# Moving the output's wait behind a branch, marking the branch on every engine, and new order tables in a graph-network kernel

## The chip, the cores and the metric

One core of a Trainium2 chip runs the kernel. The metric is the device time of one execution in microseconds, of which the median of three runs is taken. The engines are PE (matmul; its weight loads are PEld), DVE (vector), ACT (scalar), POOL (GpSimd) and SP (Sync), which issues all DMAs here.

## What is computed

128 graphs of 128 nodes with 64 features go through two layers, each followed by x + layer(x) and a layer norm.

```python
# layer 0
mask = (adj > 0.0)
h = relu((x @ W1a)[:, :, None, :] + (x[:, :, None, :] - x[:, None, :, :]) @ W1b + b1)   # H = 192
hm = einsum('bjkh,bjk->bjh', h, mask)
x = layernorm(x + hm @ W2 + deg[..., None] * b2)
# layer 1
m = relu(relu(x @ W1 + b1) @ W2 + b2)
msg = relu(einsum('bij,bjh->bih', adj, m))
gi, gh = msg @ W_ih.T + b_ih, x @ W_hh.T + b_hh          # GRU gates r, z, n
x = layernorm(x + (1 - z) * n + z * x)
```

## The kernel before

Layer 0 is done in 32 quads of four graphs (NQ = 32). For each quad q, prep builds selection words (rank_n, off, ov, rank_t, rank_ov, words), turned inputs (x_split, x_turn) and the products V (v, v_low), which Sync stores and loads again as VA and VB. A quad then goes through nine a rounds and nine b rounds. In a round PE multiplies VA or VB by a selection matrix DM (fp8, L886 and L894) into PSUM, and DVE takes the maximum with zero and adds it to AC (round_a L1184, round_b L1205; the first a round's part is on ACT). DM comes from dgen on DVE (L1163), four per step. s_ov, out0_a, out0_b and out0_c (the "tail", L959 to L988) turn AC into layer 0's output XR. Layer 1 (layer1_steps) works on units of eight graphs, the last one in two halves: squares and POOL's power for the norm, transposes (xg), m1, m2 (L702), msg (L715), gates, tanh, h, yt, the second norm and the store (L1900).

All five engines run one program each, and main_order writes down the order of the calls once for all of them; an engine takes from it those stages that it has. Step t runs round_b of quad t-1 and round_a of quad t, in turn, with 19 slots between them. What stands in a slot is written as letters in tables: p is the next piece of prep of quad t+1, r of the ranks of a group of eight graphs, t of the tail, b of POOL's add_u and scale_u, n, d and e of layer 1 units (youngest to oldest), s seeds, 0 to 3 dgen, l load, c clear, f the checks, h a conversion of biases. HEAD orders the start: there L is the first loads, X the load of XQ, W the load of bs and wa, E of w2, K of constants, G of wg, S POOL's setup, A POOL's parts of the bias, w DVE's wide_w. FIRST is step 0, ORDER the even and odd steps 1 to 30, LAST the last two, END what is left after the rounds. An engine works strictly in order, so a letter's place decides what waits behind it.

The checks (flag) count inputs for which this path doesn't hold. Their sum is cast to fi (L1317). When the five programs are through, the block ends in a barrier (L1923); each engine loads fi (L1930), and a branch runs a dense fallback over 16 groups if fi is over 0. For this input it is 0. In the profile the branch is the COMPARE_BRANCH of bacc.py:44.

```python
            sy.wait_ge(s["out"], 16 * (NG + 1))
            sy.wait_ge(s["flag"], 3)
    ...
        over = nc.values_load(fi[:], min_val=0, max_val=768)
        with nc.If(over > 0):
            with nc.Fori(0, NG) as gv:
```

Of the kernel before, what the change touches and what calls it, by code (L numbers as in the profile page):

```python
# [23 lines left out]
NG = NB // GB  # L24
# [29 lines left out]


ORDER = (
    ("se", "2pp3", "rb", "bp", "ep", "pt", "p", "bter", "p", "td", "tp", "eeeer", "d", "p", "", "ebp", "de", "c", "0r1"),
    ("slp", "2p3", "bdbbe", "", "tdb", "tp", "", "tt", "p", "ddp", "cp", "enpdr", "npd", "ddn", "p", "d", "pd", "0r1", "dp"),
)

FIRST = ("2hsp", "b3", "", "bp", "p", "", "r", "hpb", "p", "prrr", "", "bcp", "", "r", "0", "pp", "hpp", "", "1r")

LAST = (
    ("bs2bt", "", "etttn", "b3d", "", "nd", "dn", "dbd", "nd", "d", "dd", "dnde", "", "", "d", "dn", "", "n01", ""),
    ("bbetdff", "ftte2d3", "ndtnendeeeddddd", "", "df", "edbd", "nnbe", "", "d", "", "n", "en", "", "d", "", "dfen", "", "", ""),
)

HEAD = ("LSW", "Xrc", "ArE", "rKAGp", "trrrww", "pMrrt", "pppt", "p", "tfp01pp", "p", "pA")

END = ("td", "dt", "dl", "dtdtltnnn", "dllnn", "dl", "lnl", "n", "nln", "l", "l", "nnl", "ndn", "l", "n", "n", "l", "n", "nl", "n", "ll", "ntll")  # L70

MAIN = (
# [119 lines left out]
def build(nc, adj, adjt, xt, xn, xq, w1, w2, rows, wg, cst, out):  # L192
    ctx = ExitStack()
    with ctx:
# [232 lines left out]
        def finish(steps):  # L427
            for n, _ in enumerate(steps):
                assert n < 99, "waits for a bank that nothing gives back"

        def main_order(do):
# [131 lines left out]
            for t in range(NQ + 1):  # L563
                link["t"] = tail(t - 2) if t > 1 else iter(())
                link["b"] = parts_of_u(t)
                if t % 2 == 0:
                    link["e"], link["d"] = link["d"], link["n"]
                elif t > 2:
                    link["n"] = layer1_steps(do, bank, t // 2 - 1)
                if t + 1 < NQ:  # L570
                    link["p"] = prep(t + 1)
                if t % 2 and t // 2 + 2 < NG:
                    link["r"] = ranks(t // 2 + 2)
                if t == NQ:
                    link["n"] = layer1_steps(do, bank, NG - 1)
                    link["f"] = checks()
                order = FIRST if t == 0 else ORDER[t % 2] if t < NQ - 1 else LAST[t - NQ + 1]

                def between(codes):
                    for c in codes:  # L580
                        if c in "01":
                            do("dgen", t + 1, int(c))
                        elif c in "23":
                            do("dgen", t, int(c))
                        elif c == "s":
                            do("seeds", t)
                        elif c == "c":
                            do("clear", t + 1)
                        elif c == "l":
                            if t // 2 + 2 < NG:  # L590
                                do("load", t // 2 + 2)
                        else:
                            next(link[c], 0)

                between(order[0])
                for n in range(1, 10):
                    if t:
                        do("round_b", t - 1, n)
                    between(order[2 * n - 1])
                    if t < NQ:  # L600
                        do("round_a", t, n)
                    between(order[2 * n])
                finish(link["h"])
                finish(link["p"])
                finish(link["b"])
                finish(link["f"])
                finish(link["t"])
            for k in range(2):
                do("add_u", NQ - 1, k)
            link = {"t": tail(NQ - 1), "n": link["n"], "d": link["d"]}  # L610
# [152 lines left out]
        def tensor_main(e):  # L763
# [228 lines left out]
            def fsum(b, gates):  # L992
# [8 lines left out]
            follow(main_order, {"rank_n": rank_n, "off": off, "ov": ov, "rank_t": rank_t, "rank_ov": rank_ov, "x_turn": x_turn,  # L1001
                                "v": v, "v_low": v_low, "surplus": surplus, "seeds": seeds, "round_a": round_a, "round_b": round_b,
                                "s_ov": s_ov, "out0_a": out0_a, "out0_b": out0_b, "out0_c": out0_c, "fsum": fsum,
                                **tensor_layer1(e, pe, s)})
# [118 lines left out]
        def vector_main(e):  # L1123
# [195 lines left out]
            follow(main_order, {"mask": mask, "count": count, "off": off, "words": words,  # L1319
                                "dgen": dgen, "round_a": round_a, "round_b": round_b,  # L1320
                                "wide_w": wide_w, "fold": fold, "s_ov": s_ov, "add_u": add_u, "bias": bias, "flag": flag, "fsum": fsum,
                                **vector_layer1(e, ve, s)})
# [153 lines left out]
        def scalar_main(e):  # L1476
# [149 lines left out]
            follow(main_order, {"rank_n": rank_n, "split_x": split_x, "off": off, "ov": ov, "rank_t": rank_t, "rank_ov": rank_ov,  # L1626
                                "x_split": x_split, "x_turn": x_turn, "v": v, "v_low": v_low, "surplus": surplus, "seeds": seeds, "round_a": round_a, "s_ov": s_ov, "out0_c": out0_c,
                                "fold": fold, "split_x1": split_x1, "split_h": split_h,
                                **scalar_layer1(e, ac, s, 2)})
# [102 lines left out]
        def gpsimd_main(e):  # L1732
# [91 lines left out]
                if t:  # L1824
                    po.wait_ge(s["dd"], RD * t + m + 1)

            follow(main_order, {"setup": setup, "parts": parts, "count": count, "x_split": x_split, "split_x": split_x, "mask": mask, "split_xg": split_xg, "split_ms": split_ms, "split_x1": split_x1, "split_h": split_h, "s_ov": s_ov, "clear": clear, "scale_u": scale_u, "add_u": add_u, "dgen": dgen, **gpsimd_layer1(e, po, s)})

        def gpsimd_dense(e):
            follow(dense_order, gpsimd_layer1(e, Lane(e), dense))  # L1830
# [3 lines left out]
        def sync_main(e):  # L1834
# [62 lines left out]
            def store(u):  # L1897
# [4 lines left out]
            follow(main_order, {"load_x": load_x, "x_split": x_split, "load": load, "weights": weights, "weights1": weights1, "weights2": weights2, "consts": consts, "words": words, "words_b": words_b,  # L1902
                                "v_out": v_out, "v_out_b": v_out_b, "store": store})
            sy.wait_ge(s["out"], 16 * (NG + 1))
            sy.wait_ge(s["flag"], 3)

        def sync_dense(e, gv):
            sy, s = Lane(e), dense
            here = bass.ds(gv * GB, GB)

            def load(g):
                e.dma_start(AT[1][:], adj[:, here, :]).then_inc(s["dA"], 16)
                e.dma_start(AT[0][:], adjt[:, here, :]).then_inc(s["dT0"], 16)
                e.dma_start(XT, xt[:, bass.ds(gv * PG, PG), :]).then_inc(s["dA"], 16)

            def store(g):
                sy.wait_ge(s["lny"], 2)
                e.dma_start(out[:, here, :], YO[:]).then_inc(s["out"], 16)

            follow(dense_order, {"load": load, "store": store})  # L1920
            sy.wait_ge(s["out"], 16)

        with nc.Block() as block:  # L1923
            block.tensor(tensor_main)
            block.vector(vector_main)
            block.scalar(scalar_main)
            block.gpsimd(gpsimd_main)
# [63 lines left out]
```

## Time and profile before

| | us |
|---|---|
| device time, median of 3 runs | 843.34 (843.33 to 844.14) |
| device time of the profiled execution | 843.34 |
| its span, first to last instruction | 841.64 |
| PE busy | 766.6 (91%) |
| DVE busy | 746.2 (89%) |
| ACT busy | 648.3 (77%) |
| POOL busy | 539.3 (64%) |

Time stamps are microseconds from the span's start. The steps start at seeds: step 0 at 23.7, step 16 (even) at 402, step 17 (odd) at 425.5, step 18 at 451. Even steps take 23.1 us, odd ones 25.5, and this repeats from step 6 to the end. A row of a chain or a timeline is start, duration, engine, line, what is written and read, and in brackets the idle time before it with what ended it. "PEldq" and the like are an engine's sequencer: instructions that don't count as busy.

### The profile page before, as it was taken

How to read it: one execution, taken by the hardware profiler on the slowest of the kernel's cores; microseconds unless marked ns; L12 is line 12 of the kernel's file. 1: busy time of each engine (PE TensorE's matmuls, PEld its weight loads, DVE VectorE, ACT ScalarE, POOL GpSimd, SP SyncE). 2: the span in 40 equal slices, each digit the busy share in tenths (PEclk: the TensorE clock that was granted, in tenths of full speed). 3: DMA queues.
4: the chain of work that ended last, by engine and by line, in shares of the span. 5: the costliest groups of instructions: out<-in, count | busy, mean ns of one | idle time of the engine just before them, and what ended most of it. 6: DMA issues, size and time to landing. Idle time of an engine off the chain costs nothing.

```text
span 841.6 us, 25838 instructions
## 1 busy us (share of the span) xinstructions
PE 766.6 (91%) x10193; PEld 641.8 (76%) x10240; DVE 746.2 (89%) x851; ACT 648.3 (77%) x1897; POOL 539.3 (64%) x625
## 2 busy tenths in 40 slices
PE   2879899999999999999999999999999999999983
PEld 1557778788888878888887878888787888878762
DVE  3899999898999999899999989999999999998963
ACT  4746676987878798787878888787988879788562
POOL 5424445676858667685866758686775768475861
PEclk9999999999999999999999999999999999999997
DMA  5432332224233232423223242322423232131000
GB/s 173 105 103 70 88 90 77 70 58 116 59 102 80 76 83 58 120 70 97 71 76 89 57 116 70 96 71 77 106 58 98 70 96 70 43 97 42 2 13 28
DMA packets 33276, 66.17 MB, mean 79 GB/s; under 512 B 5504, under 2 KB 6272, under 8 KB 33152
## 3 DMA queue, kind: packets, MB, share of 16 engines
q1 hardware_dynamic: 33152, 64.48, 29.2%
q8 instruction: 82, 1.34, 0.7%
q14 instruction: 42, 0.34, 0.1%
HBM read 22.52 MB, written 4.19 MB: 32 GB/s over the span
## 4 chain that ended last, share of the span: by engine, by line
PE 59%; issue 15%; ACT 13%; DVE 8%; DMA 3%; POOL 1%; SPq 1%; POOLq 0%; DVEq 0%
PE PS L886 14%; PE PS L894 13%; PE PS L959 4%; PE PS L971 4%; DVE AC L1184 4%; DVE AC L1205 2%; PE PS L872 2%; PE PS L981 2%; PE PS L844 2%; DMA VA<-VN 2%; ACT AM L1516 2%; PE PS L715 2%; PE PS L702 2%; PE PS L978 1%; PE PS L878 1%
## 5 line engine op out<-in xcount | busy, mean ns | idle before, releaser
L1205 DVE SCALAR_TENSOR_TENSOR AC<-PS,AC 128x1152 f32<-128x1152 f32 (+4 forms) x288 | 334.9, 1163 | 44.8 <-PE PS L886 42.3
L1184 DVE SCALAR_TENSOR_TENSOR AC<-PS,AC 128x1152 f32<-128x1152 f32 (+4 forms) x256 | 292.4, 1142 | 13.7 <-PE PS L894 9.8
L886 PE MATMUL PS<-DM,VA 128*128 128x192 fp8e5 (+1 forms) x1024 | 121.2, 240 | 17.5 <-DVE AC L1184 5.0
L894 PE MATMUL PS<-DM,VB 128*128 128x192 fp8e5 (+1 forms) x1024 | 120.1, 240 | 14.2 <-DVE AC L1205 13.9
L886 PE MATMUL PS<-DM,VB 128*128 128x192 fp8e5 (+1 forms) x1024 | 120.6, 239 | 0.7 <-DVE AC L1205 0.2
L894 PE MATMUL PS<-DM,VA 128*128 128x192 fp8e5 (+1 forms) x1024 | 119.5, 239 | 0.6 <-DVE AC L1184 0.2
L886 PEld LDWEIGHTS PS<-DM,VA 128*128 128x128 f16 x1024 | 78.2, 98 | 51.8 <-DVE AC L1184 17.7
L1794 POOL TENSOR_TENSOR XE<-XQ,XT 128x512 f16<-128x512 f32 x32 | 40.7, 1271 | 106.6 <-ACT XT L1537 64.5
L894 PEld LDWEIGHTS PS<-DM,VB 128*128 128x128 f16 x1024 | 77.2, 98 | 32.5 <-issue 13.8
L886 PEld LDWEIGHTS PS<-DM,VB 128*128 128x128 f16 x1024 | 82.8, 98 | 2.5 <-DVE AC L1205 1.9
L894 PEld LDWEIGHTS PS<-DM,VA 128*128 128x128 f16 x1024 | 83.0, 98 | 1.7 <-DVE AC L1184 1.4
L1163 DVE TENSOR_SCALAR DM<-CW 128x1536 uint16<-128x1536 uint16 (+1 forms) x132 | 73.0, 585 | 0.9 <-DMA CW<-WM 0.9
L1820 POOL TENSOR_TENSOR AC<-AC,SD 128x512 f32<-128x512 f32 (+1 forms) x62 | 61.1, 1005 | 16.2 <-DVE DM L1163 16.2
L1813 POOL TENSOR_TENSOR SD<-SD,NNB 128x512 f32<-128x512 f32 x64 | 58.7, 917 | 1.4 <-DVE DM L1163 1.4
L1516 ACT ACTIVATE AM<-PS 64x512 int16<-64x512 f32 x64 | 37.7, 590 | 16.3 <-remote 12.5
L1687 POOL TENSOR_SCALAR st<-st 128x8 f32<-128x8 f32 (+1 forms) x17 | 3.4, 197 | 66.5 <-ACT SQ L1377 60.3
L1762 POOL TENSOR_SCALAR MT<-AT 128x1024 bf16<-128x1024 f32 x15 | 41.8, 2784 | 0.0
L971 PE MATMUL PS<-w2s,AC 128*128 128x64 f32 x256 | 40.1, 289 | 0.0
L1527 ACT ACTIVATE AM<-PS 64x256 int16<-64x256 f32 x64 | 24.2, 378 | 20.6 <-PE PS L813 20.2
L1555 ACT ACTIVATE VN<-PS 128x384 f16<-128x384 f32 x64 | 31.1, 486 | 10.7 <-PE PS L850 8.6
L1550 ACT ACTIVATE VN<-PS 128x384 f16<-128x384 f32 x64 | 30.5, 476 | 10.8 <-PE PS L844 10.7
L959 PE MATMUL PS<-w2s,AC 128*64 128x64 f32 x1024 | 36.8, 225 | 0.7
(246 smaller groups left out, 2080.4 us busy)
## 6 DMA issues: line engine op xcount, KB each, us to landing
CW<-WM SPq DMA_DIRECT2D x128, 160.0 KB, 2.8
XQ<-in_xq SPq DMA_DIRECT2D x32, 256.0 KB, 3.3
VA<-VN SPq DMA_DIRECT2D x64, 128.0 KB, 2.3
VB<-VN SPq DMA_DIRECT2D x64, 128.0 KB, 2.3
AT<-in_adjt SPq DMA_DIRECT2D x15, 512.0 KB, 3.8
XN<-in_xn SPq DMA_DIRECT2D x16, 256.0 KB, 4.1
out<-YO SPq DMA_DIRECT2D x15, 256.0 KB, 3.0
WG<-in_wg SPq DMA_DIRECT2D x1, 515.5 KB, 6.5
```

Of the source, the lines that this page charges most:

```text
L886: last = e.matmul(PS[:, b + i % 2, 256 * (i // 2) + cols.start:256 * (i // 2) + cols.stop], left(lhs, i), d[:, i, :], start=False, stop=Tr ...
L894: last = e.matmul(PS[:, b + 2, 256 * (i // 2) + cols.start:256 * (i // 2) + cols.stop], right(lhs, i), d[:, i, :], start=False, stop=True, ...
L959: last = e.matmul(PS[64 * h:64 * h + 64, b, 64 * i:64 * i + 64], ac[:, n, c:c + 64], w2s[:, w, :], start=(w == 0), stop=(w > 0))
L971: e.matmul(o, ac[:, i % 2, 256 * (i // 2) + 64:256 * (i // 2) + 192], w2s[:, 0, :], start=False, stop=True, skip_group_check=True)
L1163: e.tensor_scalar(DM[m][:, halves], CW[t % 3][:, halves, first], 6 - 2 * m, 0xC0C0, ALU.logical_shift_left, ALU.bitwise_and).then_inc(s["d ...
L1184: e.scalar_tensor_tensor(t, tiles(PS[:, b + p:b + 3, :])[:, :, cols], 0.0, t, ALU.max, ALU.add).then_inc(s["sx"], 1)
L1205: e.scalar_tensor_tensor(t, tiles(PS[:, r, :])[:, :, cols], 0.0, t, ALU.max, ALU.add).then_inc(s["sy"], 1)
L1516: e.activation(graphs(am[k])[:, :, 64 - 64 * h:192 - 64 * h], src[k], ACT.Copy, scale=2.0, bias=-258.0)
L1762: e.tensor_scalar(MT[g % 3][:], AT[g % NA][:], 0.0, None, ALU.is_gt).then_inc(s["mask"], 1)
L1794: e.tensor_tensor(XE[q % 4][:, :, nat], XQ[:], XT0[:], ALU.subtract).then_inc(s["xql"], 1)
L1813: e.tensor_tensor(u, u, NNB[:, 4 * k:4 + 2 * k, :], ALU.mult).then_inc(s["im"], 1)
L1820: e.tensor_tensor(t[:, h, nat], t[:, h, nat], SD[q % 3][:, h, :], ALU.add).then_inc(s["ad"], 1)
```

## The change

1. Sync's wait for all output stores goes from the end of its main program to the very end, behind the branch; the dense store waits for it too.
2. On each engine a place is marked ahead of the last two add_u and the END table, and the branch at the end is written out as a compare-and-branch per engine with a hint tied to that place. The kind of hint is the default, "likely taken".
3. ORDER, FIRST, LAST, HEAD and END have new letters. The number of pieces is the same, so the same work is done.

```diff
 ORDER = (
-    ("se", "2pp3", "rb", "bp", "ep", "pt", "p", "bter", "p", "td", "tp", "eeeer", "d", "p", "", "ebp", "de", "c", "0r1"),
-    ("slp", "2p3", "bdbbe", "", "tdb", "tp", "", "tt", "p", "ddp", "cp", "enpdr", "npd", "ddn", "p", "d", "pd", "0r1", "dp"),
+    ("s2b", "pp3", "bp", "", "pe", "trprbd", "", "t", "te", "tpb", "pr", "epeee", "d", "pe", "", "pc", "d", "", "e0r1"),
+    ("sp", "dp", "2b3b", "dt", "p", "bt", "t", "et", "pr", "dlendpn", "", "pdd", "dp", "dcn", "pddb", "p", "pd", "0pd1", "r"),
 )
-FIRST = ("2hsp", "b3", "", "bp", "p", "", "r", "hpb", "p", "prrr", "", "bcp", "", "r", "0", "pp", "hpp", "", "1r")
+FIRST = ("2", "spbhp", "p3", "phr", "", "", "cppb", "b", "rr", "", "", "r", "rp", "", "p", "p0b", "pp", "h", "1r")
 LAST = (
-    ("bs2bt", "", "etttn", "b3d", "", "nd", "dn", "dbd", "nd", "d", "dd", "dnde", "", "", "d", "dn", "", "n01", ""),
-    ("bbetdff", "ftte2d3", "ndtnendeeeddddd", "", "df", "edbd", "nnbe", "", "d", "", "n", "en", "", "d", "", "dfen", "", "", ""),
+    ("deesbbt2bd", "3", "tttb", "", "nd", "ndn", "nd", "d", "d", "ddd", "n", "d", "d", "n", "d", "", "n", "01", ""),
+    ("bbfe2tfdf", "ttendbdted", "fne3", "nee", "dfddndd", "d", "", "dnd", "", "n", "", "", "de", "", "", "", "dne", "en", "bed"),
 )
-HEAD = ("LSW", "Xrc", "ArE", "rKAGp", "trrrww", "pMrrt", "pppt", "p", "tfp01pp", "p", "pA")
+HEAD = ("L", "Xcrr", "SrAAEWrrK", "rrG", "tArw", "ppw", "tp", "ptpt", "p", "f", "M", "p", "ppp0p1")
-END = ("td", "dt", "dl", "dtdtltnnn", "dllnn", "dl", "lnl", "n", "nln", "l", "l", "nnl", "ndn", "l", "n", "n", "l", "n", "nl", "n", "ll", "ntll")
+END = ("tltltdn", "n", "n", "t", "ddl", "ldtln", "nnnn", "tl", "ndn", "ll", "lnnld", "l", "dd", "n", "lnlnlnn", "llnl", "ln")
...
+            do("soon")
             for k in range(2):
                 do("add_u", NQ - 1, k)
...
+            def soon():
+                hints.append((e, e.mark_branch_hint_location()))
...
-            sy.wait_ge(s["out"], 16 * (NG + 1))
             sy.wait_ge(s["flag"], 3)
...
             def store(g):
+                sy.wait_ge(main["out"], 16 * (NG + 1))
                 sy.wait_ge(s["lny"], 2)
...
+        hints = []
...
         over = nc.values_load(fi[:], min_val=0, max_val=768)
-        with nc.If(over > 0):
+        for e, soon in hints:
+            e.br_ne(over, 0, on_true="over_some", on_false="over_none").branch_hint(soon)
+        with nc.body("over_some"):
             with nc.Fori(0, NG) as gv:
...
+            nc.br("over_none")
+        nc.switch_bb("over_none")
+        nc.sync.wait_ge(main["out"], 16 * (NG + 1))
```

## Rows read from the trace of the kernel before

**Rows 1.** The page's first part: busy us, share and instructions of each engine.
```profile
PE 766.6 (91%) x10193; PEld 641.8 (76%) x10240; DVE 746.2 (89%) x851; ACT 648.3 (77%) x1897; POOL 539.3 (64%) x625
```

**Rows 2.** Sums by stretch: length, busy us of each engine, PEclk, DMA share, GB/s.
```profile
28.60:64.00 35.40, 28.24 (x340) 20.75 (x341) 35.30 (x52) 20.03 (x44) 15.31 (x20) 1.00 0.37 97
...
402.20:425.40 23.20, 21.89 (x314) 18.77 (x312) 21.58 (x23) 20.43 (x59) 19.58 (x26) 1.00 0.28 69
425.40:450.80 25.40, 24.94 (x333) 21.08 (x333) 23.34 (x24) 20.20 (x64) 14.77 (x15) 1.00 0.35 96
```

**Rows 3.** DVE's waits, 402.2 to 425.4, then 425.4 to 450.8: us, times, longest.
```profile
DVE AC L1205 <- PE PS L886: 1.6, 1, 1.6
...
DVE AC L1205 <- PE PS L886: 1.1, 2, 0.8
DVE AC L1184 <- PE PS L894: 0.6, 1, 0.6
```

**Rows 4.** The chain that ended last, 0 to 42 us: start, us, what.
```profile
3.55 6.89 DMA XQ<-in_xq
...
14.40 1.61 DVE SI L1143
...
16.70 0.70 ACT OV L1506
...
20.53 0.48 PE PS L838
...
24.29 0.46 SPq L1879
```

**Rows 5.** The block's end, L1923: sequencer operation, count, ns min/median/max, first and last start.
```profile
L1923 DVEq DRAIN  x1: 436/436/436, 834.7 to 834.7; - x1
L1923 SPq COMPARE_BRANCH  x1: 33/33/33, 836.9 to 836.9; - x1
L1923 SPq DRAIN  x1: 7/7/7, 837.0 to 837.0; - x1
```

**Rows 6.** Waits of Sync's queue, 830 to 842 us.
```profile
SPq L1923 <- DMA out<-YO: 1.3, 1, 1.3
```

**Rows 7.** The branch, bacc.py:44, two of its five engines (the others take 45, 45 and 50 ns).
```profile
bacc.py:44 DVEq COMPARE_BRANCH  x1: 72/72/72, 837.9 to 837.9; - x1
bacc.py:44 PEldq COMPARE_BRANCH  x1: 3732/3732/3732, 837.9 to 837.9; - x1
```

**Rows 8.** DMA queues from 837 to 842 us: packets, MB, share of 16 engines.
```profile
q8 instruction: 1, 0.02, 1.7%
q14 instruction: 3, 0.02, 1.7%
```

**Rows 9.** DMA queues from 812 to 820 us.
```profile
q8 instruction: 1, 0.02, 0.7%
```

**Rows 10.** Sums by stretch, 812 to 842 us.
```profile
812.00:842.00 30.00, 15.10 (x155) 11.51 (x153) 11.96 (x42) 11.87 (x44) 7.70 (x10) 0.85 0.06 20
```

**Rows 11.** Timeline of the start: start, us, engine, line, operation, in brackets idle before.
```profile
7.29 0.69 ACT L1484 ACTIVATE Q<-PS,cs 128x512 bf16<-128x512 f32 x1 [1.43 <-PE PS L773]
...
9.74 0.17 DVE L1675 TENSOR_TENSOR NVC<-CT 128x8 bf16<-128x8 f32 x1
```

**Rows 12.** DMA issues from 0 to 14 us: count, size, us from issue to landing.
```profile
XN<-in_xn SPq DMA_DIRECT2D x1, 256.0 KB, 6.1
...
bs<-in_rows SPq DMA_DIRECT2D x1, 160.0 KB, 6.7
```

**Rows 13.** Timeline from 815 to 842 us.
```profile
818.46 0.15 DVE L1317 CAST fi<-PS 1x1 int32<-1x1 f32 x1 [2.25 <-PE PS L998]
818.47 1.65 POOL L1697 TENSOR_TENSOR st<-st 128x8 f32<-128x8 f32 x1
...
818.99 0.42 DVE L1065 TENSOR_REDUCE st<-X 128x4 f32<-128x256 f32 x1
```

**Rows 14.** Timeline of an odd step, 424.5 to 442 us.
```profile
431.69 1.15 PE L959 MATMUL PS<-w2s,AC 128*64 128x64 f32 x32
...
432.67 1.05 PE L715 MATMUL PS<-AT,M 128*64 128x128 f32 x16
```

More of the change, by code:

```diff
@@ L999, in fsum @@
                 last.then_inc(s["fsum"], 1)
-            follow(main_order, {"rank_n": rank_n, "off": off, "ov": ov, "rank_t": rank_t, "rank_ov": rank_ov, "x_turn": x_turn,
+            def soon():
+                hints.append((e, e.mark_branch_hint_location()))
+            follow(main_order, {"soon": soon, "rank_n": rank_n, "off": off, "ov": ov, "rank_t": rank_t, "rank_ov": rank_ov, "x_turn": x_turn,
                                 "v": v, "v_low": v_low, "surplus": surplus, "seeds": seeds, "round_a": round_a, "round_b": round_b,
@@ L1317, in fsum, with soon @@
                 e.tensor_copy(fi[:], PS[0:1, b, 0:1]).then_inc(s["flag"], 1)
-            follow(main_order, {"mask": mask, "count": count, "off": off, "words": words,
+            def soon():
+                hints.append((e, e.mark_branch_hint_location()))
+            follow(main_order, {"soon": soon, "mask": mask, "count": count, "off": off, "words": words,
                                 "dgen": dgen, "round_a": round_a, "round_b": round_b,
@@ L1624, in fold, with soon @@
                     e.activation(JK[:, 0:F], wbt[:, k, :], ACT.Square, accum_out=wst[:, 4 + k:5 + k]).then_inc(s["cn"], 1)
-            follow(main_order, {"rank_n": rank_n, "split_x": split_x, "off": off, "ov": ov, "rank_t": rank_t, "rank_ov": rank_ov,
+            def soon():
+                hints.append((e, e.mark_branch_hint_location()))
+            follow(main_order, {"soon": soon, "rank_n": rank_n, "split_x": split_x, "off": off, "ov": ov, "rank_t": rank_t, "rank_ov": rank_ov,
                                 "x_split": x_split, "x_turn": x_turn, "v": v, "v_low": v_low, "surplus": surplus, "seeds": seeds, "round_a": round_a, "s_ov": s_ov, "out0_c": out0_c,
@@ L1825, in dgen, with soon @@
                     po.wait_ge(s["dd"], RD * t + m + 1)
-            follow(main_order, {"setup": setup, "parts": parts, "count": count, "x_split": x_split, "split_x": split_x, "mask": mask, "split_xg": split_xg, "split_ms": split_ms, "split_x1": split_x1, "split_h": split_h, "s_ov": s_ov, "clear": clear, "scale_u": scale_u, "add_u": add_u, "dgen": dgen, **gpsimd_layer1(e, po, s)})
+            def soon():
+                hints.append((e, e.mark_branch_hint_location()))
+            follow(main_order, {"soon": soon, "setup": setup, "parts": parts, "count": count, "x_split": x_split, "split_x": split_x, "mask": mask, "split_xg": split_xg, "split_ms": split_ms, "split_x1": split_x1, "split_h": split_h, "s_ov": s_ov, "clear": clear, "scale_u": scale_u, "add_u": add_u, "dgen": dgen, **gpsimd_layer1(e, po, s)})
         def gpsimd_dense(e):
@@ L1900, in store, with soon @@
                 e.dma_start(out[:, g * GB + c.start:g * GB + c.stop, :], YO[:, c, :]).then_inc(s["out"], 16)
-            follow(main_order, {"load_x": load_x, "x_split": x_split, "load": load, "weights": weights, "weights1": weights1, "weights2": weights2, "consts": consts, "words": words, "words_b": words_b,
+            def soon():
+                hints.append((e, e.mark_branch_hint_location()))
+            follow(main_order, {"soon": soon, "load_x": load_x, "x_split": x_split, "load": load, "weights": weights, "weights1": weights1, "weights2": weights2, "consts": consts, "words": words, "words_b": words_b,
                                 "v_out": v_out, "v_out_b": v_out_b, "store": store})
-            sy.wait_ge(s["out"], 16 * (NG + 1))
             sy.wait_ge(s["flag"], 3)
```

## Prediction

> **What bounds the kernel now.** I read the page first: PE is busy 91% and DVE 89% of an 841.6 us span [rows 1]. Neither share says which engine to watch, so next come the sums by stretch [rows 2]. From 28.6 to 64 us DVE is busy 35.30 of 35.40 us: the first step is a solid row of DVE work, and whatever lets it begin earlier moves everything behind it. In the repeating pair of steps an even step (402.2 to 425.4) has 1.6 us of DVE idle, an odd one (425.4 to 450.8) has 2.1 us, while PE is busy 24.94 of 25.40. So even steps hang on DVE, odd ones on PE. The DVE waits say the same: one wait of 1.6 us at the head of the even step, for the first b round, and in the odd step waits on PE [rows 3]. Last come the two ends, where no engine is full. The start is a chain of DMA, ACT and DVE steps up to the first store of V at 24.29 us [rows 4]; the finish is a chain of short operations, ended by the block's barrier, a wait for the output, a register load and a branch [rows 5 to 7].
>
> **The base of the sum.** The profiled execution is one with a device time of 843.34 us, and the median of the three runs is the same 843.34. Its span is 841.64, so 1.70 us lie outside the span; I keep them as they are.
>
> **Part 1, the output's wait moved behind the branch.** Sync queues the last store at 835.1 and is then held 1.3 us at the block's end by "DMA out<-YO" [rows 6]; only then does its DRAIN at 837.0 let the barrier go, and all five engines load the flag [rows 5]. Without this wait the barrier needs DVE's DRAIN, which begins at 834.7 and takes 436 ns (to 835.17) [rows 5], and Sync's own end of issue at about 835.5. Its wait for the flag was met long before, when DVE wrote fi at 818.5 [rows 13]. So barrier, load and branch move up by 1.3 us: minus 1.3, almost sure. What is late next is the same output: its wait ended at 836.9 [rows 5], and Sync must still wait for it. Sync's branch, at 838.1 before, comes at 836.8, so the wait ends some 0.1 us behind it and costs nothing more. Behind the moved wait nothing is queued but the end of the program. The dense path gets a wait too, but this data never enters it (the branches are followed by no dense instruction).
>
> **Part 2, the branch marked.** The branch out of the main part takes 45 to 72 ns on four engines and 3732 ns on PE's sequencer, and with it the span ends (837.9 + 3.73 = 841.64) [rows 7]. In the same stretch instruction packets move: one of q8 and three of q14 [rows 8]. q8 carries PE's code: 82 packets over the span, for the 10193 matmuls and 10240 weight loads of the profile's first table, one packet per 249 instructions. So the 3.7 us are code that PE waits for, as the target lies behind the whole dense body. If the mark brings this code in early, PE's branch costs what it costs elsewhere, about 0.07. With part 1 PE then branches at 836.6, Sync at 836.85, and the output's wait ends the span at about 836.95. Parts 1 and 2 together: 841.64 minus 836.95, 4.7 us. If the mark does nothing, the gain is 1.3. The mark itself adds one sequencer instruction per engine; the nearest rows are the 7 ns DRAIN and the 72 ns branch [rows 5, 7], all on engines that here wait for one another: 0 to 0.1, I take 0.
>
> What speaks against the mark is where it stands: before the END table, at about 812 us. PE still has over 250 matmuls and weight loads to go [rows 10], and a next packet of q8 falls in that stretch, one between 812 and 820 [rows 9]. A block fetched for the branch has to survive this. The Trainium skill, page "Runtime: NRT & Kernel Launch", section "Instruction fetch mechanics", says that the instruction memory is only two cache lines with sequential prefetch, and that a taken branch outside the window waits for a fetch. The trace agrees with the wait (3.73 us); no run yet shows what an early mark does. By that rule taken strictly the early block is displaced and the gain is the 1.3 us of part 1 alone; that is rival B below.
>
> **Part 3, the HEAD table.** Before, ACT runs Q (7.29), then waits for XQ (3.55 plus 6.89, so 10.44) to do x_split, then rank_t's AM, XHL and JK, and only then the copy VE, for which DVE stands idle until SI at 14.40 [rows 4, 11]. NVC, the end of DVE's count, is done at 9.9 [rows 11], and the product that VE copies comes out of that count. The new table has split_x and off of ranks (the letters r) ahead of rank_t (t) and x_split (p). XN was queued fourth, at 2.12, and took 6.1 [rows 12]: landed at 8.2. Then XHL 0.63 and JK 0.8 on ACT end near 9.7, VE at 9.8, SI on DVE from about 10.0 instead of 14.40. OV follows behind AM (about 2.0) and x_split (0.63), at about 12.4 instead of 16.70: 4.3 earlier. What is late next is POOL: bs is now queued behind XQ and the w2 load, so the parts start near 10.3 instead of 9.33; parts one and two cost 0.71+0.24+0.40+0.67+0.40+0.67 = 3.1, XHL's low half 1.15, part three 0.4, XE 1.15, together 16.1. (bs: queued at 2.60, 6.7 to landing [rows 12], and one 256 KB and one 160 KB load more ahead of it.) The first V product then goes at about 16.2 to 16.5 against 20.53 [rows 4], some 4 us earlier. DVE's fold and the first dgen, which used to fill gaps, must fit in the shorter head: DVE has 13.7 us of work in the first 30, so they fit, but may cost some tenths. I take 3.5 at the head, with 0 (it is all given back) and 4.5 (all of OV's lead) as ends. It carries over to the end because DVE is full from 28.6 to 64 [rows 2].
>
> **Part 4, END.** On POOL the pow of the last full unit's second norm (1.65 at 818.47) [rows 13] stands ahead of the first norm of the last half unit, whose sums DVE had ready at 819.41; it starts at 820.20 [rows 13]. New order: out0_a to out0_c (t) go ahead of most of d's steps. At best this gives back the 0.8 us; at worst the d steps on ACT (16 SY operations, 2.03) fall in front of the longer chain. I take 0.5 earlier, ends 1.5 earlier and 1.0 later.
>
> **Part 5, the step tables.** ORDER runs in 30 steps, 15 odd and 15 even, so each tenth of a microsecond per step is 3 us. Even: one dgen moves ahead of b1 into the 1.6 us hole. b1 itself waits for seeds on PE, which runs without a gap from the last a round to b1, and b2 follows b1 over PE, so this fills idle time only: 0 to 0.15 per step. The rest of the even step is DVE work without holes. Odd: the m2 product (L702, 1.05) goes from behind the first a round to before it, and msg (L715, 1.05) and s_ov (L959, 1.15 from 431.69) go from behind a2 to before it [rows 14]. By the issue times that is 0.98 + 0.97 = 1.95 us of PE between b2 and a2: DVE, done with b2 at 432.42, would find a2 at 433.5 and stand 1.1 us. The old 0.8 ahead of b3 and 0.6 ahead of a3 [rows 3] shrink for it, as PE's total is unchanged and PE is the bound: net 0, between 0.3 less and 0.6 more. The same work in other slots on both sides, so I take 0 for ORDER, FIRST and LAST together, ends 6 less and 9 more.
>
> **Sum.** 843.34 - 4.7 - 3.5 - 0.5 + 0 = 834.6 us.
>
> **Rivals.** B: the mark does not bring PE's code (displaced by q8's next packet, or the mark is for the other side of the branch). For it: the packet between 812 and 820 [rows 9], and that nothing in the trace shows a mark at work. Against: PE waits idle for long stretches near the end, with the queue free. Price 3.4: 838.0.
> C: the head's gain is lost, since POOL's parts, XHL and XE now stand in a row and bs lands later; the first step starts where it did. For it: the POOL chain above. 843.34 - 4.7 - 0.5 = 838.1.
> D: the step tables pay too, 0.2 us in each of 30 steps, for the 3.7 us of DVE idle per pair: 834.6 - 6 = 828.6.
> E: slower. In odd steps m2, msg and s_ov ahead of the early a rounds make DVE stand and PE's total isn't made good, because a3 and b4 then wait in turn on DVE. Price up to 1.1 per odd step; it decides from 8.7/15 = 0.58 of it kept. At 0.8 kept, 12 us: 846.6. Against it: PE is full in odd steps anyway.
>
> **Chances.** Forecast 0.50, B 0.20, C 0.12, D 0.10, E 0.08. Range for 8 in 10: from 829.5 (half of D's gain and the head's upper end) to 840.0 (B or C with 2 us of tables against it). About 0.2% (1.7 us) is what a measurement of this kernel can tell from no change. Faster by more: all of the forecast, D, and B and C but for 0.05 in which the tables cost another 4 us: 0.87. Same 0.05. Slower 0.08, E.
>
> **What will show it.** PE's branch: 3732 ns before; under 200 if the mark works. The wait on "DMA out<-YO" after the flag load instead of at the block's end. SI's first start near 10 instead of 14.40, the first VA store near 20 instead of 24.29. The 48.6 us of a pair of steps, and DVE's idle ahead of a2 in odd ones. The prediction is wrong if a pair is off by over 0.3 us, if PE's branch stays long, or if DVE's full stretch still starts at 28.6.

## The result

The changed kernel takes 835.54 us, the median of four runs (834.79 to 836.19), against 843.60 for the kernel before (843.33 to 844.14), the ratio being 0.9903 with an interval of 0.9891 to 0.9916. That is 8.1 us or 1.0% faster. The forecast was 834.6 with a range of 829.5 to 840.0. The profiled execution of the changed kernel has a device time of 836.19 and a span of 834.72 us, so 1.47 us lie outside the span (before 1.70).

In the changed kernel most lines have moved by a few: L872 is L873, L886 L887, L894 L895, L959 L960, L1143 L1147, L1163 L1167, L1184 L1188, L1205 L1209, L1923 L1940; the branch is L1949, and Sync's last wait for the output L1963.

### The profile after

The page's first part, which answers [rows 1], and from the page's groups the line of dgen (out<-in, count, busy us, mean ns, idle before it):

```profile
PE 771.7 (92%) x10240; PEld 644.1 (77%) x10240; DVE 760.6 (91%) x851; ACT 643.1 (77%) x1897; POOL 544.5 (65%) x625
...
L1167 DVE TENSOR_SCALAR DM<-CW 128x1536 uint16<-128x1536 uint16 (+1 forms) x132 | 87.9, 688 | 1.0 <-DMA CW<-WM 1.0
```

DVE has the same 851 instructions and is 14.4 us busier than before (760.6 against 746.2 [rows 1]), in a kernel that is faster. The growth is that of dgen, whose mean was 585 ns and 73.0 us in sum on the page before. More on that below.

Sums by stretch, with the columns of [rows 2]:

```profile
26.70:60.70 34.00, 27.04 (x316) 19.65 (x314) 33.79 (x50) 18.71 (x42) 14.69 (x19) 1.00 0.40 111
399.70:423.00 23.30, 21.98 (x310) 18.83 (x311) 22.57 (x24) 20.06 (x59) 19.95 (x26) 1.00 0.27 66
423.00:448.40 25.40, 25.19 (x334) 21.28 (x335) 23.66 (x24) 20.35 (x65) 15.00 (x15) 1.00 0.35 98
```

DVE's full row of the first step starts at 26.7 instead of 28.6. The pair of steps from 399.7 to 448.4 is 48.7 us long, where it was 48.6 [rows 2].

DVE's waits in these two steps, the even one and then the odd one (us in total, times, longest):

```profile
DVE AC L1209 <- PE PS L887: 0.7, 2, 0.6
...
DVE AC L1188 <- PE PS L895: 1.1, 1, 1.1
DVE AC L1209 <- PE PS L887: 0.6, 3, 0.2
```

The 1.6 of the even step [rows 3] has become 0.6. In the odd step the 0.8 and the 0.6 [rows 3] are gone, and 1.1 stands ahead of a2 instead.

The start, on DVE's timeline (start, us, line, operation, in brackets the idle time before) and one line of ACT's:

```profile
9.42 1.23 DVE L1147 TENSOR_TENSOR SI<-cs,VE 128x1024 bf16<-128x1024 bf16 x1
15.45 1.14 DVE L1217 COPY br<-bp 1x192 bf16<-1x192 bf16 x1 [2.02 <-POOL bp L1762]
26.75 1.02 DVE L1182 SCALAR_TENSOR_TENSOR AC<-PS,AC 128x384 f32<-128x384 f32 x2 [2.50 <-PE PS L887]
...
12.21 0.69 ACT L1513 ACTIVATE OV<-PS,cs 128x512 bf16<-128x512 f32 x1
```

SI starts at 9.42 (14.40 before) and OV at 12.21 (16.70 before [rows 4]). The chain that ended last, from 0 to 42 us, shows what came in their place:

```profile
3.54 6.33 DMA bs<-in_rows
9.96 1.24 POOL SD L1759
...
13.97 1.11 POOL XHL L1799
15.08 0.35 POOL bp L1762
15.45 0.50 DVE br L1217
15.96 0.57 issue
17.73 0.48 PE PS L839
```

This chain has no SI, OV or XQ before the first V product. It runs from the load of bs over POOL's parts to DVE's copies of the bias rows, and then to the product at 17.73 (20.53 before [rows 4]).

Last, the end: the block's barrier (L1940), the branch (L1949) and Sync's last wait (L1963), with the columns of [rows 5]:

```profile
L1940 DVEq DRAIN  x1: 436/436/436, 831.9 to 831.9; - x1
L1940 SPq COMPARE_BRANCH  x1: 78/78/78, 832.7 to 832.7; - x1
L1940 SPq DRAIN  x1: 7/7/7, 833.1 to 833.1; - x1
L1949 DVEq COMPARE_BRANCH  x1: 90/90/90, 834.0 to 834.0; - x1
L1949 PEldq COMPARE_BRANCH  x1: 402/402/402, 834.0 to 834.0; - x1
L1949 SPq COMPARE_BRANCH  x1: 65/65/65, 834.2 to 834.2; - x1
L1963 SPq EVENT_SEMAPHORE  x1: 17/17/17, 834.7 to 834.7; - x1
```

PE's branch takes 402 ns where it took 3732 [rows 7]. DVE's DRAIN begins 1.2 us ahead of Sync's; before it was 2.3 us ahead (834.7 and 837.0 [rows 5]).

### Where the time went

I cut both spans at three events: the start of the first seeds product (L872 before, L873 after) of the third step, the same of the last step, and the end of DVE's last write. The times are the starts and ends of these instructions in the two traces, each span being one profiled execution:

| stretch | before | after | difference |
|---|---|---|---|
| start to seeds of the third step | 63.7 | 60.7 | -3.0 |
| from there to seeds of the last step | 702.9 | 704.9 | +2.0 |
| from there to DVE's last write | 68.5 | 66.7 | -1.8 |
| from there to the end of the span | 6.53 | 2.40 | -4.1 |
| span | 841.6 | 834.7 | -6.9 |

The tail gives most, then the start, then the last step. The loop gives nothing and loses 2.0 of one execution: 0.8 in one odd step (26.5 us between seeds instead of 25.7), 1.1 in the second last step (24.2 instead of 23.1), which the LAST table orders; the rest are small changes of both signs that cancel. The profiled execution of the changed kernel is the slowest of its four (836.19; the others have spans of 833.3 to 834.0), so the 6.9 is less than the usual gain.

### The profile page after: what moved, and what is told of

The parts are those of the page before. It is cut to its first block, busy times and chain, and to the rows that moved or that the text cites. A ratio compares the mean times of both kernels' runs of the same rounds, so it can differ in the third digit from the quotient of the medians.

```text
span 834.7 us, 25918 instructions
## 1 busy us (share of the span) xinstructions
PE 771.7 (92%) x10240; PEld 644.1 (77%) x10240; DVE 760.6 (91%) x851; ACT 643.1 (77%) x1897; POOL 544.5 (65%) x625
## 4 chain that ended last, share of the span: by engine, by line
PE 65%; issue 17%; DVE 11%; ACT 3%; DMA 2%; POOL 1%; SPq 0%; DVEq 0%; POOLq 0%; ACTq 0%
PE PS L887 16%; PE PS L895 15%; DVE AC L1188 5%; DVE AC L1209 4%; PE PS L972 4%; PE PS L960 4%; PE PS L873 3%; PE PS L982 2%; PE PS L716 2%; PE PS L879 2%; PE PS L703 2%; DMA VA<-VN 1%; PE PS L979 1%; PE PS L845 1%; PE PS L655 1%
## 5 line engine op out<-in xcount | busy, mean ns | idle before, releaser
L1209 DVE SCALAR_TENSOR_TENSOR AC<-PS,AC 128x1152 f32<-128x1152 f32 (+4 forms) x288 | 334.9, 1163 | 28.8 <-PE PS L887 28.3
L1188 DVE SCALAR_TENSOR_TENSOR AC<-PS,AC 128x1152 f32<-128x1152 f32 (+4 forms) x256 | 292.1, 1141 | 16.3 <-PE PS L895 15.7
L895 PE MATMUL PS<-DM,VB 128*128 128x192 fp8e5 (+1 forms) x1024 | 120.0, 240 | 15.9 <-DVE AC L1209 14.8
L887 PE MATMUL PS<-DM,VA 128*128 128x192 fp8e5 (+1 forms) x1024 | 121.1, 240 | 13.9 <-DVE AC L1188 5.6
L887 PE MATMUL PS<-DM,VB 128*128 128x192 fp8e5 (+1 forms) x1024 | 120.4, 239 | 0.6 <-DVE AC L1209 0.2
L895 PE MATMUL PS<-DM,VA 128*128 128x192 fp8e5 (+1 forms) x1024 | 119.5, 239 | 0.7 <-DVE AC L1188 0.2
L895 PEld LDWEIGHTS PS<-DM,VB 128*128 128x128 f16 x1024 | 79.1, 98 | 38.4 <-issue 17.9
L887 PEld LDWEIGHTS PS<-DM,VA 128*128 128x128 f16 x1024 | 77.1, 99 | 39.7 <-DVE AC L1188 18.5
L1167 DVE TENSOR_SCALAR DM<-CW 128x1536 uint16<-128x1536 uint16 (+1 forms) x132 | 87.9, 688 | 1.0 <-DMA CW<-WM 1.0
L1830 POOL TENSOR_TENSOR AC<-AC,SD 128x512 f32<-128x512 f32 (+1 forms) x62 | 65.2, 1064 | 30.5 <-DVE DM L1167 30.5
L887 PEld LDWEIGHTS PS<-DM,VB 128*128 128x128 f16 x1024 | 82.9, 98 | 2.2 <-DVE AC L1209 1.6
L895 PEld LDWEIGHTS PS<-DM,VA 128*128 128x128 f16 x1024 | 82.9, 98 | 1.8 <-DVE AC L1188 1.7
L1534 ACT ACTIVATE AM<-PS 64x256 int16<-64x256 f32 x64 | 24.2, 378 | 21.8 <-PE PS L814 20.7
L1611 ACT ACTIVATE XR<-PS 128x256 f32<-128x256 f32 x32 | 12.3, 384 | 36.7 <-PE PS L989 36.7
L1588 ACT ACTIVATE AC<-PS 128x1152 f32<-128x1152 f32 (+1 forms) x32 | 35.4, 1107 | 2.2 <-PE PS L895 2.1
```

The costliest lines, as they stand in the source:

```text
L887: last = e.matmul(PS[:, b + i % 2, 256 * (i // 2) + cols.start:256 * (i // 2) + cols.stop], left(lhs, i), d[:, i, :], start=False, stop=Tr ...
L895: last = e.matmul(PS[:, b + 2, 256 * (i // 2) + cols.start:256 * (i // 2) + cols.stop], right(lhs, i), d[:, i, :], start=False, stop=True, ...
L1167: e.tensor_scalar(DM[m][:, halves], CW[t % 3][:, halves, first], 6 - 2 * m, 0xC0C0, ALU.logical_shift_left, ALU.bitwise_and).then_inc(s["d ...
L1188: e.scalar_tensor_tensor(t, tiles(PS[:, b + p:b + 3, :])[:, :, cols], 0.0, t, ALU.max, ALU.add).then_inc(s["sx"], 1)
L1209: e.scalar_tensor_tensor(t, tiles(PS[:, r, :])[:, :, cols], 0.0, t, ALU.max, ALU.add).then_inc(s["sy"], 1)
L1588: e.activation(ac_[:, 2 * p:6, front], tiles(PS[:, b + p:b + 3, :])[:, :, front], ACT.Relu).then_inc(s["sx"], 1)
```

## Experiments

All twelve were timed against the kernel before on the same chip. "Old" and "new" tables are those before and after the change. Where a kernel has no hint, it still has the same written-out branches and differs in the hint alone. A difference in microseconds is worked out from the ratio, on 843.6 us; where the two medians give something else by 0.2 us or more, that stands beside it. Each such difference is uncertain by 0.8 to 1.3 us.

### The two halves of the tail

The first kernel has all old tables and no mark; only Sync's wait moves.

```diff
-            sy.wait_ge(s["out"], 16 * (NG + 1))
             sy.wait_ge(s["flag"], 3)
...
+        nc.switch_bb("over_none")
+        nc.sync.wait_ge(main["out"], 16 * (NG + 1))
```

> The kernel before with the output's wait alone moved behind the branch; old tables, the branch written out per engine without a hint. Theory T (the tail is barrier, flag load, then PE waiting for code): barrier, load and branch come 1.3 us earlier, PE's branch keeps its 3.7 us, span 841.6 - 1.3 = 840.3. Rival R (the 3.7 us at PE's branch are bound to the output's landing or to a fixed end of the program, not to code): 841.6 unchanged.

Measured: 841.83 us, ratio 0.9982 (0.9973 to 0.9991), which is 1.5 us less. Its barrier, branch and last wait:

```profile
L1940 SPq COMPARE_BRANCH  x1: 38/38/38, 835.2 to 835.2; - x1
L1940 SPq DRAIN  x1: 7/7/7, 835.4 to 835.4; - x1
L1949 PEldq COMPARE_BRANCH  x1: 3607/3607/3607, 836.3 to 836.3; - x1
```

The drain is at 835.4 instead of 837.0 [rows 5], PE's branch is nearly as long as before and starts 1.6 earlier. 0.3 of this is no gain of the change: DVE's last write, which comes ahead of it all, was 0.3 earlier in this execution. The rest is the 1.3 of the wait, as expected.

The second kernel has the old tables and the old wait, and the mark and hint on all five engines.

```diff
+            do("soon")
...
-        with nc.If(over > 0):
+        for e, soon in hints:
+            e.br_ne(over, 0, on_true="over_some", on_false="over_none").branch_hint(soon)
```

> The kernel before with the marks and hints alone, the output's wait left ahead of the block's end. T: PE's branch falls from 3.73 to about 0.4 us as in the changed kernel; the span ends with PE's or Sync's branch near 838.3, so 3.3 less. R: no gain, or PE's branch stays at 3.7.

Measured: 840.68 us, ratio 0.9964 (0.9951 to 0.9978), 3.0 us less (2.7 between the medians). Sync's wait of [rows 6] and the lines of its end:

```profile
SPq L1940 <- DMA out<-YO: 1.3, 1, 1.3
...
L1940 SPq COMPARE_BRANCH  x1: 78/78/78, 836.6 to 836.6; - x1
L1949 PEldq COMPARE_BRANCH  x1: 402/402/402, 837.9 to 837.9; - x1
```

The hint alone takes 3.33 us off PE's branch (3732 to 402 ns), and 3.4 off the span (838.3). The time shows that much within its uncertainty.

The third has both, with the old tables.

```diff
-            sy.wait_ge(s["out"], 16 * (NG + 1))
...
+            do("soon")
+        for e, soon in hints:
+            e.br_ne(over, 0, on_true="over_some", on_false="over_none").branch_hint(soon)
+        nc.sync.wait_ge(main["out"], 16 * (NG + 1))
```

> Wait moved and hints, all five tables old. T: 4.1 less (the two traces put the time from DVE's last write to the end at 6.53 before and 2.40 after), so 837.5 span, 839.2 device; the rest of the change's 8 us then belongs to the tables. If the two parts simply add up, w_only and h_only give 1.3 and 3.3, together 4.6; the moved wait ends the span instead, which takes back some 0.5.

Measured: 838.85 us, ratio 0.9942 (0.9929 to 0.9956), 4.9 us less (4.5 between the medians) and a span of 837.4. The single parts give 1.5 and 3.0, so they add up within the uncertainty: each removes a piece of the same chain, barrier and branch. The prediction had 4.7.

### Does an early mark survive?

Rival B rested on PE's next code packet displacing the block that the mark had brought in. If so, a mark at the very start of the program must be worthless. This kernel has both parts of the tail and the old tables, and the marks of all five engines stand ahead of their first work.

```diff
+            do("soon")
             for c in "".join(HEAD):
...
-            do("soon")
             for k in range(2):
                 do("add_u", NQ - 1, k)
```

> As both_tail, but the marks stand at the very start of the program, so that some 80 packets of PE's code pass between mark and branch. T with a hint that is kept until its branch: same time as both_tail, PE's branch about 0.4. Rival (a block fetched for the mark at once is displaced by the next packets): PE's branch is back at 3.7 and the time 3 us above both_tail, or code is fetched again and again and some of the stream's packets come late.

Measured: 838.26 us, ratio 0.9936 (0.9922 to 0.9950), not distinguishable from the mark near the end. PE's branch:

```profile
L1949 PEldq COMPARE_BRANCH  x1: 402/402/402, 835.6 to 835.6; - x1
```

Some 80 packets of PE's code queue passed between mark and branch (the whole span has 81), and the branch costs the same 402 ns. So nothing displaces what the mark does.

The packets also say what is different at the branch. From the start to 830 us the queue q8 has moved 81 packets in the kernel with the wait alone (no hint), and 81 as well in the two hinted ones, with the mark near the end and at the start. While PE's branch runs, the kernel with no hint (836.2 to 839.9 us) shows

```profile
q14 instruction: 3, 0.02, 2.5%
q8 instruction: 1, 0.02, 2.1%
```

and the hinted ones show no packet at all (836.6 to 837.3 and 835.5 to 836.4 us). So PE's long branch is a time in which a packet of its code comes in, and the hint takes this packet away. But it isn't moved to an earlier time: between mark and branch a hinted kernel has no packet of q8 more than the other. That the mark brings the target's code in early, as the prediction had it, is therefore not what these packets show; how the hint does without the packet stays open.

### Head, ORDER, LAST and END apart

Each of these three has the old tail, no hints, and the new text of the named tables only.

```diff
-HEAD = ("LSW", "Xrc", "ArE", "rKAGp", "trrrww", "pMrrt", "pppt", "p", "tfp01pp", "p", "pA")
+HEAD = ("L", "Xcrr", "SrAAEWrrK", "rrG", "tArw", "ppw", "tp", "ptpt", "p", "f", "M", "p", "ppp0p1")
```

> The kernel before with the new HEAD table alone. Theory T (the head's lead is kept because DVE is full in the first step): seeds of step 1 at 37.8 instead of 40.7 and the whole time 2.9 less, 840.5. Rival R (new HEAD and new FIRST only work together, since the old FIRST has the bias conversions late): the first step takes more than 16.7 and under 1.5 us is left, 842.

Measured: 840.18 us, ratio 0.9966 (0.9954 to 0.9979), 2.9 us less (3.4 between the medians). The first seeds start at 20.9 instead of 24.0, those of the last step at 763.0 instead of 766.6: what the start gives is still there at the end. Rival C is out.

```diff
 ORDER = (
-    ("se", "2pp3", "rb", "bp", ...
-    ("slp", "2p3", "bdbbe", "", ...
+    ("s2b", "pp3", "bp", "", ...
+    ("sp", "dp", "2b3b", "dt", ...
 )
```

> The kernel before with the new ORDER table alone. T (the same PE and DVE work in other slots): the pair of steps stays at 48.6 and the time within 1 us, 843.3. Rival S (the 2.0 us that the changed kernel lost between the seeds of steps 1 and 31 belong to this table): 845.3, with a first odd step of 26.6 instead of 25.7 and even steps over 23.2. Rival U (they belong to the earlier start, which puts loads in each other's way): as before, no 26.6.

Measured: 843.79 us, ratio 1.0003 (0.9994 to 1.0012). The one long odd step is here too: 26.5 us, where the kernel before has 25.7. DVE's waits in it with the new table (133 to 161 us) and with the old (133 to 160 us):

```profile
DVE AC L1188 <- PE PS L895: 2.5, 2, 1.4
DVE AC L1209 <- PE PS L887: 1.0, 4, 0.3
```

```profile
DVE AC L1205 <- PE PS L886: 1.3, 3, 0.8
DVE AC L1184 <- PE PS L894: 0.9, 2, 0.6
```

In this step DVE waits 3.5 us against 2.2, and the step is 0.8 longer. All later odd steps take 25.4 us with the new table and 25.5 with the old. One of them, with the new table (425.1 to 450.5 us):

```profile
DVE AC L1188 <- PE PS L895: 1.0, 1, 1.0
DVE AC L1209 <- PE PS L887: 0.6, 3, 0.2
```

Rival E falls: its stand ahead of a2 is there, the waits of 0.8 and 0.6 [rows 3] are gone for it, and DVE waits 1.6 us in all where it waited 1.7. Rival D, a gain in every step, falls as well: a pair of steps takes 48.6 us with either table.

```diff
 LAST = (
-    ("bs2bt", "", "etttn", ...
+    ("deesbbt2bd", "3", "tttb", ...
...
-END = ("td", "dt", "dl", "dtdtltnnn", ...
+END = ("tltltdn", "n", "n", "t", ...
```

> The kernel before with the new LAST and END tables alone. T: from the seeds of step 31 to DVE's last write 66.7 us as in the changed kernel instead of 68.5, so 1.8 less, 841.5. Rival (the gain comes from what ORDER hands over): no gain, 843.3.

Measured: 841.93 us, ratio 0.9982 (0.9973 to 0.9991), 1.5 us less (1.7 between the medians). The last step's seeds start 1.1 later than before (767.7 against 766.6), and from there to DVE's last write there are 66.2 us instead of 68.5. The sums of these last stretches, the kernel before first, then this one:

```profile
766.60:835.10 68.50, 57.36 (x644) 43.88 (x643) 49.54 (x103) 41.66 (x142) 40.59 (x42) 0.99 0.07 21
```

```profile
767.70:833.90 66.20, 55.94 (x636) 42.78 (x633) 47.84 (x101) 40.24 (x139) 40.20 (x40) 0.99 0.05 18
```

DVE's waits for POOL's norms in these stretches, before:

```profile
DVE X L1071 <- POOL st L1689: 3.8, 2, 2.2
DVE YO L1117 <- POOL st L1697: 2.4, 2, 1.5
```

and with the new tables:

```profile
DVE YO L1121 <- POOL st L1707: 1.1, 1, 1.1
```

The waits on POOL fall from 6.2 us to 1.1, but this isn't the gain. DVE's idle time in the stretch falls only from 19.0 to 18.4 us (68.50 less 49.54, and 66.20 less 47.84), as other waits grow: the longest is now one of 3.8 us on PE's b round (L887). The rest of the 2.3 us is work that the new LAST has put ahead of this stretch (DVE is busy 1.7 less in it), for which the step before is 1.1 longer. What part 4 was about did come: POOL does the first norm of the last half unit (L1699) ahead of the second norm of the unit before (L1707), where it had them the other way round [rows 13].

```profile
818.68 1.02 POOL L1699 TENSOR_TENSOR st<-st 128x4 f32<-128x4 f32 x1
...
821.12 1.64 POOL L1707 TENSOR_TENSOR st<-st 128x8 f32<-128x8 f32 x1
```

Before, that first norm stood at 820.48, behind the other, and both were in the chain that ended last; now only L1707 of the two is. How much of the 1.5 us this order gives was not shown. END and LAST were not run apart from each other, so which of the two tables does it is open too.

Two more put one old table back into the changed kernel.

```diff
-FIRST = ("2", "spbhp", "p3", "phr", ...
+FIRST = ("2hsp", "b3", "", "bp", ...
```

> The changed kernel with the old FIRST table. If new FIRST is worth something on the new HEAD (bias conversions in the head's gap), 0.3 to 0.5 us more; if it is worth nothing, the changed kernel's 835.5; if it costs (the late first steps seen with old ORDER, 18.3 instead of 16.3), up to 1 less.

Measured: 835.82 us, ratio 0.9919 (0.9906 to 0.9933). The changed kernel's interval is 0.9891 to 0.9916: the two overlap, so FIRST is worth nothing that can be told here, and 1 us could hide in them.

```diff
 ORDER = (
-    ("s2b", "pp3", "bp", "", ...
-    ("sp", "dp", "2b3b", "dt", ...
+    ("se", "2pp3", "rb", "bp", ...
+    ("slp", "2p3", "bdbbe", "", ...
 )
```

> The changed kernel with the old ORDER table. S (ORDER costs): 2 us faster than the changed kernel, 833.5. T (ORDER is worth nothing, the 2.0 us of that one profile are chance of its loads): the changed kernel's 835.5. U: as T, with its 26.6 step kept.

Measured: 835.08 us, ratio 0.9899 (0.9884 to 0.9914), the same as with the new ORDER. This run settles more than that. The mean of a dgen on its page is 580 ns, as before, against 688 in the changed kernel. DVE gets back the 15 us that the new ORDER costs it, and the kernel is no faster.

### Which engines need the hint?

First, hints on PE, DVE and ACT only, the rest as in the changed kernel. Its aim was Sync: the changed kernel's barrier jump on Sync (L1940) takes 78 ns and its drain follows some 0.4 us later; with no mark on Sync the nearest rows are 38 ns and 0.2.

```diff
-            e.br_ne(over, 0, on_true="over_some", on_false="over_none").branch_hint(soon)
+            branch = e.br_ne(over, 0, on_true="over_some", on_false="over_none")
+            if soon is not None:
+                branch.branch_hint(soon)
```

> The changed kernel with marks and hints on PE, DVE and ACT only; POOL and Sync branch without one. Theory T (Sync's hint costs time: its jump to the block's barrier takes 0.37 us with a mark armed and 0.17 without, and its wait behind the branch starts 0.52 us after the branch instead of 0.18): barrier 0.2 earlier, last wait at about 834.1 instead of 834.7, so 0.5 less than the changed kernel. Rival V (Sync's or POOL's code isn't near, and they then wait for it): 1 to 3 us more.

Measured: 834.97 us, ratio 0.9903 (0.9888 to 0.9918), the changed kernel's own.

```profile
L1940 SPq COMPARE_BRANCH  x1: 33/33/33, 833.1 to 833.1; - x1
L1940 SPq DRAIN  x1: 7/7/7, 833.3 to 833.3; - x1
```

Sync's jump is quick again (0.2 us to the drain instead of 0.4), so an armed mark does slow another jump on its engine. But Sync's last wait still ends about half a microsecond after its branch (834.82, the branch being at 834.3), though the output had landed at 834.44. In the changed kernel it is 834.70, with the output there from 834.07. I had blamed Sync's hint for this too; that is wrong. The half microsecond is there in every kernel with the moved wait and a hint, the one with the hint on PE alone included (832.8 and 833.3), and in the kernel with the wait alone it is 0.2 (836.5 and 836.6). The cause stays open.

Then the hint on PE alone, in the same way.

> The changed kernel with a mark and hint on PE alone. Theory F (DVE and ACT fetch their code too, hidden so far under PE's longer wait; in the trace with no hints two packets of q14 leave with PE's own): the span looks as short as hint3's, but the device time lies further above the span, by 1 to 2 us. Rival G (only PE's target is far): the same as hint3.

Measured: 839.22 us, ratio 0.9953 (0.9939 to 0.9966): 3.7 us slower than the changed kernel and 4.2 slower than hint3, both between medians. Yet the span of its profiled execution is the shortest but one of all:

```profile
core 0: 833.3 us, clock 0.997
...
L1949 DVEq COMPARE_BRANCH  x1: 72/72/72, 832.6 to 832.6; - x1
L1949 PEldq COMPARE_BRANCH  x1: 407/407/407, 832.6 to 832.6; - x1
```

Nothing in these rows is slow. But in all five executions 3.8 to 4.2 us lie outside the span, where every other kernel here has 1.4 to 2.0. Something that lies behind the last recorded instruction costs 2.5 us more, and it comes and goes with the hints of DVE and ACT: hint3 differs from this kernel in those two alone and has 1.5 outside. (The other 1.7 us between the two medians lie in the spans, which go from 833.3 to 835.8 here and from 833.3 to 834.8 in hint3. Nothing in the profiled executions explains them.)

The trace's DMA packets go on behind the span. From 834 to 838 us, with the span over at 833.3, this kernel has one packet left, in q14, the trace's other queue of instruction packets beside PE's q8:

```profile
q14 instruction: 1, 0.01, 0.7%
```

It starts at 836.5, 2.6 us behind the last one ahead of it. In hint3, whose span is over at 834.8, no packet starts behind 835.7. In the kernel with the wait alone, which has no hint, the like packet starts at 839.8, inside the span, while PE's branch still lasts until 839.9. So code that DVE or ACT waits for after its branch fits: it is hidden behind PE's 3.6 us as long as PE has no hint. Which of the two engines the packet is for, the trace doesn't say.

### A combination

The old ORDER and FIRST, with the new HEAD, LAST and END, the moved wait, and the hint on three engines.

```diff
+    ("se", "2pp3", "rb", "bp", ...
+    ("slp", "2p3", "bdbbe", "", ...
...
+FIRST = ("2hsp", "b3", "", "bp", ...
...
+            if soon is not None:
+                branch.branch_hint(soon)
```

> New HEAD, LAST and END, old FIRST and ORDER, hints on PE, DVE and ACT. If parts add: changed kernel 835.5, less 0.5 for Sync's hint, less 0.4 for the old ORDER: 834.6.

Measured: 834.77 us, ratio 0.9905 (0.9890 to 0.9920). Its profiled execution has the shortest span of all (833.0), but its time isn't distinguishable from the changed kernel's. I claim nothing for it but that ORDER and FIRST can stay old.

## Why the prediction was right

| part | predicted | alone (interval) | read from |
|---|---|---|---|
| 1 and 2, the tail | -4.7 | -4.9 (-6.0 to -3.7) | both halves together |
| of it part 1 | -1.3 | -1.5 (-2.3 to -0.8) | the wait alone |
| 3, HEAD | -3.5 | -2.9 (-3.9 to -1.8) | HEAD alone |
| 4, END | -0.5 | -1.5 (-2.3 to -0.8) | LAST and END together |
| 5, ORDER | 0 | +0.3 (-0.5 to +1.0) | ORDER alone |
| sum | -8.7 | -9.0 | |
| the whole change | | -8.2 (-9.2 to -7.1) | |

That the forecast lies within 1 us of the result is partly luck: the head is 0.6 too high and the last step 1.0 too low. The parts' sum and the whole differ by 0.8 us, which is inside what four such measurements leave uncertain (about 1.9 us).

**Part 1** held by its own steps. The wait left the block's end, the barrier then hung on DVE's DRAIN and Sync's issue, and the moved wait came to its place behind the branch. It should have ended about 0.1 us behind Sync's branch, and in the kernel with the wait alone it ended 0.2 behind it. Only with the hints did it end 0.5 behind, with the output landed up to 0.6 us before.

**Part 2** held in what it is worth: PE's wait for code goes away. That the mark brings this code in early isn't shown, and the packets speak against it. Its terms were too small in two places. PE's branch was to cost what it costs elsewhere, 0.07, and under 200 ns was named as the sign; it costs 0.40. This costs nothing here, as PE is through at 834.4 and Sync's wait ends the span at 834.7. And the mark was costed at nothing, while Sync's other jump takes 0.2 us longer with a mark armed. Together with Sync's late wait that puts the end of the span 2.4 us behind DVE's last write where the prediction's steps give 1.8 (836.95 less 835.11 of before). In the spans the tail is thus worth 4.1 and not 4.7.

Against the mark stood the rule of the Trainium skill, page "Runtime: NRT & Kernel Launch", section "Instruction fetch mechanics": two lines of code memory, sequential prefetch, a fetch for a taken branch outside them. By that rule alone the gain would have been 1.3. The run with the mark at the start shows the opposite for a hinted branch; for one with no hint the rule and the 3.6 us agree. Rival B deserved less than 0.2, though nothing in the trace of before could have said so.

**Part 3**: SI and OV came as worked out (9.42 and 12.21 against 10.0 and 12.4). The load of bs landed at 9.87 against 10.3. POOL's first part then took 1.24 us against 0.71, its last one ended at 15.4 where the prediction's terms give 14.95, and XE at 16.5 against 16.1. What failed is the step from there to the V product: it was put at 16.2 to 16.5 and came at 17.73. In between stand six copies of the bias rows on DVE (L1217 and L1218), from 15.45 to 17.63. In the head before they were over by 19.24, with the product at 20.53 waiting for something else, and so the prediction didn't count them as part of POOL's chain. The new order makes them part of it. The first copy took 1.14 us, with POOL's XE running beside it (15.38 to 16.53), and a later one of the same shape 0.20. The first store of VA, put near 20, came at 21.5. The gain carried through to the end, as said.

**Part 4** is the term that was sized worst. The order on POOL changed as forecast, and 0.5 was put on it; LAST and END together give 1.5, just at the end of its range. The prediction had put LAST at nothing, within part 5, and no run tells the shares of the two tables.

**Part 5** came out as worked: the stand ahead of a2, put at 1.1, is 1.06 in the trace, the old 0.8 and 0.6 went for it, and the pair kept its length.

```profile
429.30 1.34 DVE L1209 SCALAR_TENSOR_TENSOR AC<-PS,AC 128x1152 f32<-128x1152 f32 x1
431.71 1.36 DVE L1188 SCALAR_TENSOR_TENSOR AC<-PS,AC 128x1152 f32<-128x1152 f32 x1 [1.06 <-PE PS L895]
```

The argument was that PE is full and the moves change nothing in its sum; DVE's 15 extra microseconds, found only afterwards, tested this harder than the moves did. What the argument missed are two steps at the seams, where one table's step follows another's: 0.8 us in an odd step with the new ORDER (26.5 in the ORDER run too, 25.7 in all with the old), and 1.1 in the first step of LAST (24.2 in every kernel with the new LAST, 23.1 to 23.2 without). The first was made good elsewhere, the second inside the last step.

## What to carry to other kernels

When the last instructions are a barrier and a branch over a large body, look at what each sequencer pays for the branch, and take the wait for the output out of the barrier; here that gave more than the new table of a long loop, which gave nothing. Hint the branch on every engine that pays for it (here PE, and DVE or ACT), and compare the device time as well as the span, since the span may end ahead of what an engine without a hint still pays. In a head that is a chain, write down the next chain to its last copy before sizing the gain.

## What the runs showed of the hardware

- **A hinted branch.** 3.6 to 3.7 us with no hint and 0.40 with one on PE, the same with the mark some 80 code packets earlier. With no hint one packet of PE's code queue falls into the branch, with a hint none, and none is added ahead of it. On DVE it is 90 ns with the hint and 72 without, on Sync 65 and 50.
- **A cost outside the span.** With a hint on PE alone 3.8 to 4.2 us lie between span and device time, against 1.5 with DVE and ACT hinted as well, and a last instruction packet starts 3.2 us behind the span's end.
- **An armed mark isn't free.** Sync's barrier jump takes 78 ns against 33 to 38, and the drain behind it starts 0.2 us later.
- **DVE beside POOL.** In the changed kernel the 124 dgen of 1536 elements fall into two kinds: 84 take 0.55 us each and have POOL at work in 26% of their time, and 40 take 1.04 us with POOL at work in 86% of it, in operations with two tensor inputs. Before, 12 of the 124 were long (0.91 us). The timeline has both engines side by side; the two dgen in it are 0.83 us each:

```profile
427.34 1.16 POOL L1804 TENSOR_TENSOR XE<-XQ,XT 128x512 f16<-128x512 f32 x1 [3.65 <-ACT XT L1544]
427.72 1.66 DVE L1167 TENSOR_SCALAR DM<-CW 128x1536 uint16<-128x1536 uint16 x2
```

The new ORDER puts more dgen beside such POOL work. That is the source of DVE's extra 15 us (40 by 1.04 and 84 by 0.55 make 87.8, where 12 by 0.91 and 112 by 0.55 made 72.5), which the old ORDER gives back. This would fit the Trainium skill, page "GPSIMD Engine Reference", section "Specifications", by which GpSimd shares its SBUF interfaces with VectorE, with contention where VectorE's instruction has two SBUF inputs or is in a 2-port perf mode. dgen has one input, and no run here shows its mode; that POOL's reads are the cause was not tested by a run of its own either.
